# Attention and experts in one kernel: the barrier between the two parts taken out, the experts' start moved into the last batch

## What is computed

```python
x = L0_attn_x                                   # (8, 1024, 256)
xn = _layernorm(x, axis=-1)
# attention: a second layer norm of xn with ln_w, ln_b, 16 heads of 16, rotary q and k
scores = jnp.einsum('bhqd,bhkd->bhqk', q, k) / jnp.sqrt(jnp.float32(hd))
attn = jax.nn.softmax(scores, axis=-1)
out = jnp.einsum('bhqk,bhkd->bhqd', attn, v)
attention = xn + out.transpose(0, 2, 1, 3).reshape(B, N, D) @ Wo.T + bo
# experts: each of 8 experts takes its 256 best rows of each batch
affinity = jax.nn.softmax(jnp.einsum('bsd,de->bse', xn, gate_w), axis=-1)
gating, index = jax.lax.top_k(jnp.transpose(affinity, (0, 2, 1)), K)
h = jax.nn.silu(x_sel @ Wg[e]) * (x_sel @ Wu[e])          # x_sel: the rows taken, of xn
x_out = jnp.zeros_like(xn).at[b_idx, index].add((h @ Wd[e]) * gating[..., None])
return x + attention + x_out
```

## Time and profile before

| what | value |
|---|---|
| time, median of 3 runs | 1924.89 us (1923.93 to 1927.3) |
| time of the profiled execution | 1923.88 us |
| its span in the trace | 1922.1 us |
| PE busy (share of the span) | 90% |
| ACT busy | 62% |
| DVE busy | 56% |
| POOL busy | 34% |
| mean granted TensorE clock | 0.96 of full speed |

### The profile page before, as it was taken

The page is one execution under the profiler, slowest core; times in us unless marked ns, Lnnn a source line. Parts: engine busy times, 40 slices in busy tenths (PEclk is TensorE's granted clock), DMA queues, the critical chain, the costliest instruction groups (busy, mean ns, idle before and its releaser), DMA issues. The chain is left out here.

```text
span 1922.1 us, 28864 instructions
## 1 busy us (share of the span) xinstructions
PE 1730.4 (90%) x11240; PEld 1016.0 (53%) x11240; DVE 1085.6 (56%) x1910; ACT 1185.1 (62%) x1390; POOL 662.6 (34%) x599
## 2 busy tenths in 40 slices
PE   2469999999999999999999998872999999999997
PEld 2323434434433444444444343232888888888886
DVE  8846457556656555654655757822545545554543
ACT  0048887887887888788788889961333333333332
POOL 3333123233132133123213311003465565556553
PEclk9669999999999999999999999995999999999999
DMA  3173475476467458447547546423344344344333
GB/s 95 66 157 64 118 151 107 104 165 132 97 162 142 95 141 150 110 125 151 125 119 152 130 98 124 70 71 103 80 91 91 61 97 89 60 96 94 57 60 33
DMA packets 115250, 203.42 MB, mean 106 GB/s; under 512 B 21008, under 2 KB 59280, under 8 KB 115088
## 3 DMA queue, kind: packets, MB, share of 16 engines
q1 hardware_dynamic: 83600, 142.48, 34.1%
q0 software_dynamic: 31488, 58.74, 14.9%
HBM read 116.22 MB, written 84.93 MB: 105 GB/s over the span
## 5 line engine op out<-in xcount | busy, mean ns | idle before, releaser
L607 ACT ACTIVATE probs<-score 128x1024 f32<-128x1024 f32 x1024 | 979.3, 1026 | 227.2 <-PE score L745 227.1
L759 PE MATMUL o_ps<-probs,v_ones 128*32 128x512 f32 x4096 | 505.3, 612 | 0.9 <-ACT probs L607 0.9
L745 PE MATMUL score<-q_stack,k_stack 50*128 50x512 f32 x2048 | 399.8, 460 | 50.1 <-ACT probs L607 40.8
L745 PEld LDWEIGHTS score<-q_stack,k_stack 50*128 50x128 f32 x2048 | 164.9, 187 | 365.0 <-ACT probs L607 298.6
L1302 ACT ACTIVATE silu<-g_ps 128x512 f32<-128x512 f32 x128 | 76.5, 598 | 333.6 <-PE g_ps L1336 333.6
L1262 POOL DMA_INDIRECT out<-y,rows_now x128 | 203.7, 1591 | 206.1 <-DVE y L1415 176.8
L759 PEld LDWEIGHTS o_ps<-probs,v_ones 128*32 128x32 f32 x4096 | 107.8, 110 | 239.4 <-issue 162.6
L542 POOL TENSOR_TENSOR square<-qk 128x512 bf16<-128x512 f32 x64 | 88.2, 1407 | 368.8 <-DVE qk L896 368.8
L1404 DVE TENSOR_TENSOR h<-u_ps,silu 128x512 f32<-128x512 f32 x128 | 88.5, 691 | 209.7 <-PE u_ps L1336 184.8
L1253 POOL DMA_INDIRECT xs<-xn_rows,rows_now x128 | 131.7, 1029 | 38.0 <-issue 29.2
L513 POOL TENSOR_SCALAR ve<-mv 128x4 f32<-128x4 f32 x32 | 7.5, 235 | 307.3 <-DVE mv L816 307.3
(11 more groups left out here) (173 smaller groups left out, 2856.9 us busy)
## 6 DMA issues: line engine op xcount, KB each, us to landing
q_parts<-parts SPq DMA_DIRECT2D x16, 1024.0 KB, 4.3
k_parts<-parts SPq DMA_DIRECT2D x16, 1024.0 KB, 6.9
q_stack<-q_parts SPq DMA_DIRECT2D x64, 256.0 KB, 7.3
k_stack<-k_parts SPq DMA_DIRECT2D x64, 256.0 KB, 9.6
xin<-in_x POOLq DMA_DIRECT2D x16, 512.0 KB, 6.2
xn_rows<-xn POOLq DMA_DIRECT2D x16, 512.0 KB, 4.7
out<-xin POOLq DMA_DIRECT2D x16, 512.0 KB, 3.8
q_stack<-q_parts SPq DMA_DIRECT2D x64, 128.0 KB, 8.2
```

The lines of the kernel that those rows point to most:

```text
L607: act.activation(probs[probs_of(s)][:, 2 * i:2 * i + 2, :], score[ring_of(p)][:, :, :], ACT.Exp, scale=SCALE).then_inc(exp_done, 1)
L745: last = pe.matmul(score[ring_of(p)][:, w, :], k_stack[par][rows, i, kt * P:(kt + 1) * P], q_stack[par][rows, i, qh * HALF:(qh + 1) * HALF ...
L759: last = pe.matmul(o_ps[j * KEYS_W:(j + 1) * KEYS_W, :], v_ones[par][:, kt, j, :], probs[probs_of(s)][:, j, :], start=kt == 0, stop=kt == ...
```

## The change

Both parts become one function, `program`, with one block, so the engines no longer meet in the middle. The experts' tiles become views of attention tiles that are dead by then, and their PSUM banks are the attention's: `g_ps`, `u_ps`, `xt_ps` are the halves of `score` 0, 1 and 2, `d_ps` is `o_ps` and `side`. What the experts need first is put into the last batch: SP loads the first expert's weights there, ACT makes their high parts in cycles 20 to 22 and DVE the low parts in cycles 28 to 30, DVE converts the lists in cycle 25, PE transposes them as the extra job of cycle 27, and POOL gathers units 0 and 1. Batch 7's last four output projections are put at the ends of units 0 and 1. The arithmetic is the same.

```diff
-    LAST_JOBS = {0: ("top",), 9: ("wo", 0), 15: ("wo", 1), 23: ("wo", 2), 30: ("wo", 3)}
+    LAST_JOBS = {0: ("top",), 9: ("wo", 0), 15: ("wo", 1), 23: ("wo", 2), 27: ("lists",), 30: ("wo", 3)}
+    WEIGHT_CYCLE = (20, 21, 22)
+    LISTS_CYCLE = 25
+    LOW_CYCLE = (28, 29, 30)
+    END_BANKS = {("wo", q): (q // 2, q % 2) for q in range(QUARTERS)}
...
@@ SP: in the last batch, after store_o(b, 2) @@
+            else:
+                sp.wait_ge(base_out, 2 * DMA * NB)
+                sp.wait_ge(xn_out, 2 * DMA * NB)
+                sp.wait_ge(side_free, jobs.base)
+                load_weights(0)
...
@@ SP: behind the last batch @@
         load_den(NB - 1, 1)
         load_base(NB - 1)
+        sp.wait_ge(w_split, WEIGHTS)
+        load_weights(1)
         load_num(NB - 1, 1)
         spread_rec(NB - 1, 1)
         for hf in range(2):
             store_y(NB - 1, hf, end_jobs)
+        for e in range(2, E):
+            sp.wait_ge(w_split, WEIGHTS * e)
+            load_weights(e)
...
@@ POOL: behind the last batch @@
         attend(NB - 1, None, NB - 2)
+        pool.wait_ge(base_out, 2 * DMA * NB)
+        pool.wait_ge(xn_out, 2 * DMA * NB)
+        pool.wait_ge(parts_ready, 2 * NB)
+        pool.wait_ge(top_spread, 2)
+        pool.wait_ge(side_free, last_jobs.done(("lists",)))
+        gather(0)
+        gather(1)
         divide(NB - 1, 0)
-        divide(NB - 1, 1)
+        for unit in range(E * UNITS):
+            if unit + 2 < E * UNITS:
+                gather(unit + 2)
+            if unit == 0:
+                divide(NB - 1, 1)
+            scatter(unit)
...
@@ POOL: in scatter @@
+            if e == 0:
+                pool.wait_ge(y_out, 2 * DMA * (2 * bp + 2))
...
@@ ACT: in the last batch, and behind it @@
+                for m in range(WEIGHTS):
+                    if nxt is None and s == 2 * WEIGHT_CYCLE[m] + 1:
+                        act.wait_ge(side_free, last_jobs.base)
+                        high_weights(0, m)
...
+        act.wait_ge(parts_out, NB * 2 * PARTS_DMA)
+        turned(0)
+        act.wait_ge(pv_done, NB * STEPS)
+        for unit in range(E * UNITS):
+            expert_unit(unit)
...
@@ PE: behind the last batch @@
-        for s in (STEPS - 2, STEPS - 1):
-            weigh(NB - 1, s)
-        for job in END_JOBS:
-            pe.wait_ge(side_free, end_jobs.before(job))
-            run_job(end_jobs, job, None, NB - 1, side[:, :])
+        weigh(NB - 1, STEPS - 2)
+        turn(0)
+        weigh(NB - 1, STEPS - 1)
+        for unit in range(E * UNITS):
+            if unit % UNITS == 0:
+                pe.wait_ge(w_split, WEIGHTS * (unit // UNITS + 1))
+            gate_up(unit)
+            if unit + 1 < E * UNITS:
+                turn(unit + 1)
+            if unit == 0:
+                pe.wait_ge(o_copied, NB * 2 * NG)
+                pe.wait_ge(side_free, end_jobs.base)
+            down(unit)
+            for job in END_JOBS:
+                if END_BANKS[job][0] == unit:
+                    pe.wait_ge(x_split, DC * (unit + 1) + END_BANKS[job][1] + 1)
+                    run_job(end_jobs, job, None, NB - 1, xt_ps[END_BANKS[job][1]])
...
@@ DVE: in the last batch, and behind it @@
+                    if c == LISTS_CYCLE:
+                        order_lists()
...
+                if nxt is None and c in LOW_CYCLE:
+                    if c == LOW_CYCLE[0]:
+                        dve.wait_ge(parts_out, NB * 2 * PARTS_DMA)
+                    low_weights(0, LOW_CYCLE.index(c))
...
         copy_o(NB - 1, 2 * NG - 1)
-        for qh in range(2):
-            if qh == 1:
-                invert(NB - 1, 1)
-            for i in range(2):
-                quarter_split(NB - 1, 2 * qh + i)
-            for i in range(2):
-                take(end_jobs, ("wo", 2 * qh + i), None, NB - 1, side[:, :])
+        turned(0)
+        for unit in range(E * UNITS):
+            expert_unit(unit)
...
@@ DVE: in expert_unit @@
+                if unit == 0 and f == 1:
+                    invert(NB - 1, 1)
+            low(unit, FC - 1)
+            if unit + 1 < E * UNITS:
+                turned(unit + 1)
+            if unit < 2:
+                quarter_split(NB - 1, 2 * unit)
+                quarter_split(NB - 1, 2 * unit + 1)
...
@@ the new helpers that these call @@
+        def low_weights(e, m):
+            dve.wait_ge(w_high, WEIGHTS * e + m + 1)
+            dve.tensor_tensor(we_lo[e % 2][m], w_raw[m], we_hi[e % 2][m], ALU.subtract).then_inc(w_split, 1)
...
+        def high_weights(e, m):
+            act.wait_ge(w_in, WEIGHTS * DMA * (e + 1))
+            act.copy(we_hi[e % 2][m], w_raw[m]).then_inc(w_high, 1)
...
+        def turn_lists(bank):
+            pe.wait_ge(row_added, 3)
+            for i, src in enumerate((row_f, gate_f)):
+                for half in range(HALVES):
+                    at = (HALVES * i + half) * LISTS
+                    last = pe.transpose(bank[:, at:at + LISTS], src[:, half * P:(half + 1) * P], ident_sb[:, :])
+            return last
```

463 lines of the change are left out of this document (191 added, 272 removed).

## The result

The changed kernel took 1880.96 us (median of 4 runs, 1877.44 to 1884.39) beside 1926.1 us of the kernel before (1923.93 to 1928.88): a ratio of 0.976, 95% interval 0.9742 to 0.9778. The forecast was 1876 us, with a range of 1871 to 1885. The median fell by 45.1 us; the sum had said 48.6. (The kernel before has one more run here than it had at the forecast, when its median was 1924.89 us.) In the profiled executions, which can be taken apart, the span fell by 42.9 us, 5.7 short of the sum. The join was forecast to the tenth of a microsecond. Of the 5.7 us, 2.5 lie in the batches ahead of it, 2.5 in the units from unit 3 on, 0.5 in unit 0 and 0.4 in units 1 and 2; the smaller terms gave back 0.3.

What follows compares the result with a forecast made beforehand. PE was taken to bound the kernel, busy 90% of 1922.1 us, except in the 57.0 us join. Terms summed to -48.6 us, giving a 1873.5 us span, 1875.3 with the time around it, forecast as 1876 (range 1871 to 1885).

Steps and rivals of the forecast that it cites:

- the sum: All terms added: -57.0 + 2.1 + 2.6 + 5.8 - 2.15 + 0.1 = -48.6 us.
- The join: Between last `weigh` and first gate matmul: 57.0 us taken out, 2.1 us of DVE's copy and low parts left.
- The casts: ACT's three weight casts in cycles 20 to 22 of the last batch: 2.6 us added, between 2.4 and 2.94.
- The output projections: Four projections moved onto PE's path at the ends of units 0 and 1: 5.8 us added.
- The clock at unit 0: Unit 0 starts at full clock after the short hole, taking 17.65 us instead of 19.80: -2.15 us.
- a short fall of the clock: Rival: PE begins unit 0 at half clock after the 2.1 us hole, costing 2.15 us, so 1878; chance 0.13.
- A unit takes 17.65 us: Expert units from unit 3 on: the prediction is wrong if any takes anything but 17.65 us.
- a wait of PE for a split in units 0 to 3: Sign in the first expert units: if PE waits for a split there, the prediction is wrong.
- The batches ahead: Attention batches before the join: no change forecast; about half of 1.0 us added for the profiled execution lying below the median.
- The queues: Second half's way round beside units 0 and 1, with POOL and DVE work queued behind: costed at nothing.
- backed-up queues: Rival in units 0 to 3: slow transfers and a late chain cost PE 2 to 9 us, 1878 to 1885; chance 0.14.
- The late rows: Rival: the first gather starts only at the last batch's end, 8.5 to 11 us back, 1884 to 1886; chance 0.06.

Runs made afterwards that it cites:

- late gather: Changed kernel with POOL's first gather of expert rows waiting until PE has done all weighs of the last batch but the last: 1894.08 us, ratio 0.9831.
- 160 bytes: Changed kernel with 160 bytes of padding per partition behind zn_lo, run twice: 1881.19 us (ratio 0.9759) and 1879.22 us (0.9737).
- 416 bytes: Changed kernel with 416 bytes of padding per partition behind zn_lo: 1877.4 us, ratio 0.974 to the kernel before.
- 32 bytes: Changed kernel with 32 bytes of padding ahead of the second tile of parts, which holds the rows, and 32 behind it: 1884.74 us, ratio 0.9775.
- control: The changed kernel itself, unedited, run once more beside three edited kernels on one chip: 1878.54 us, ratio 0.9752.

## Why the forecast was nearly right, step by step

**The join, -57.0 and +2.1 us.** Right, both to 0.1 us. The three pieces of the gap (0.07, 0.69, 1.28 and the reaction) were those of the earlier trace rows. The two kernels with another order on DVE show that most of the gap was not needed: 0.74 us is left when `copy_o` is out of it.

**The casts, +2.6 us.** The number came out, 2.47 us between the same marks in the profiles compared, but with luck. From the mark to the end of the last `weigh`, the nine kernels with the casts on ACT and no late gather fall into two kinds. Three of them took 131.0 us, with the clock at 1.00 throughout. Six, the changed kernel among them, took 131.9 to 132.5 us, and in each the clock fell once while the casts ran. The three with the casts on POOL took 129.5 to 129.6 us and the kernel before 129.40, none with a fall. So the casts themselves cost 1.4 to 1.6 us, under the forecast's lower end of 2.4, and a fall of the clock beside them another 0.9 to 1.5. The same 20 us in the changed kernel and in the changed kernel again (columns as in the earlier trace rows):

```profile
1239.00:1259.00 20.00, 17.90 (x118) 6.62 (x112) 13.26 (x30) 18.85 (x21) 0.00 (x0) 0.91 0.04 9
1239.00:1259.00 20.00, 17.62 (x128) 6.51 (x120) 14.79 (x34) 19.41 (x21) 0.00 (x0) 1.00 0.06 14
```

The step that was wrong is the wait that the casts absorb: the forecast allowed 0.54 us of it. In the changed kernel run again ACT stood idle for 8.1 us from the mark to the last `weigh`, against 9.0 in the kernel with POOL's casts and no padding. That is 0.9 us of waits absorbed. The rest of the difference was not traced. Whether the casts bring the fall about isn't shown either; it came in seven of the ten profiles with casts on ACT, the late gather included, and in none of the four without. One `cast` itself took 1.05 us, about as in the earlier trace rows:

```profile
1242.11 1.05 ACT L706 CAST zn_hi<-xin 128x1024 fp32r<-128x1024 f32 x1
1243.05 3.78 ACT L737 ACTIVATE probs<-score 128x1024 f32<-128x1024 f32 x4
1246.67 1.08 ACT L706 CAST zn_hi<-xn 128x1024 fp32r<-128x1024 f32 x1
```

**The output projections, +5.8 us.** Right: the pair behind unit 0 took 2.84 us, 5.7 us for the four, and doubling them added 5.5 in the profile. `turn(1)` to `turn(3)` grew by 6.24 us all the same: the rest is 0.4 us of slower even experts and the 0.2 us that PE lost behind DVE's low part.

**The clock at unit 0, -2.15 us.** The direction was right and the size was not. `gate_up(0)` gave back 1.64 us in the profiled execution; it would have been 1.90 but for the 0.26 us that an even expert's `gate_up` now takes more. Part of the miss is a reading of the rows. The chain's row of unit 1 starts at 1362.83 us, but PE's timeline of the kernel before has that first gate matmul at 1362.67. Unit 0 had lost 1.99 us there (12.90 - 10.91), not 2.15. And the fall came back in some profiles: of the nine with a gap of 2.1 us and no late gather, three show it (12.6 to 12.8 us to `turn(1)` instead of 11.0 to 11.3). That is the rival "a short fall of the clock", which had 0.13: it came true in a third of the profiles, at about 1.6 us. In neither profile with a gap of 0.74 us did it fall. The nine are of seven kernels. Both profiles with 160 bytes alone have the fall and neither of the changed kernel does, so whether it goes by the execution or by the edit isn't shown. The Trainium skill ("TensorE: Matmul & The Clock Gate", section "What's actually happening") says that the same kernel can see the change at another place in another run. The two profiles of the changed kernel agree in batch 7 and ahead of it: the first has a fall beside the casts and a long batch 6, the second has neither.

**"A unit takes 17.65 us": the term that was mis-sized.** The forecast named it as what would prove it wrong. Units of even experts took 17.82 to 17.92 us. `gate_up` of an even expert took 0.26 us more (11.17 - 10.91), the unit as a whole about 0.18, since what is behind `gate_up` took 6.66 us there and 6.74 in the others. `turn(3)` to `turn(31)`, with 13 such units, is 2.5 us longer than before, and with units 0, 1 and 2 it comes to some 3.0 us. The other sign that was named, a wait of PE for a split in units 0 to 3, came true too, by the 0.7 us in `down(1)`. The cause is where tiles lie in memory: in the joined program weights and rows share the attention's tiles, and the gate matmuls have a pitch of 227 ns if both kinds lie at the same place modulo 256 bytes, and of 232 to 233 ns at the other distances tried. Three edits that only move tiles show it from both sides: 160 or 416 bytes made the slow units fast, 32 bytes made the fast ones slow. How the chip comes to it stays open. `parts0`, which holds two of the six parts of an even expert's weights (one of the four that `gate_up` reads), was at the same place modulo 256 as the rows in the changed kernel, and its matmuls were followed after 234 and 235 ns, as slow as those beside them. So it isn't a matter of one matmul's own two operands. Nor are all matmuls of a slow expert slow: by their place in a slice the means over its units at full clock go from 226.5 to 237.3 ns.

**The batches ahead, +2.5 us.** The forecast took the profiled execution of before as the base and added half a microsecond. Nothing was changed there, and the mark of the same program stood at 1159.15 and at 1155.87 us. The stretch ahead of it goes in steps: from a batch to the next it is 147.1 us, or about 1.65 or 3.3 us more. The granted clock goes with it: in a batch of 147.1 us it fell to half speed for a short while once, in one of 148.8 twice, in one of 150.4 three times. These are batches 2, 4 and 6 of the changed kernel, and batch 6 of the kernel before (from first `weigh` to first `weigh`; PE's busy time alone):

```profile
416.40:567.10 150.70, 145.33 (x994) 0.97 0.58 129
715.80:862.90 147.10, 142.02 (x990) 0.99 0.57 129
1010.20:1160.60 150.40, 146.03 (x995) 0.97 0.56 125
```

```profile
1010.80:1158.10 147.30, 142.91 (x998) 0.99 0.59 129
```

Batch 6 is where the changed kernel lost what it lacks at the mark: 150.4 us against 147.3. Over the fourteen profiles the time from the first `weigh` of batch 1 to the mark goes from 883.7 us with 8 such falls to 894.3 us with 14, some 1.7 us for each. What sets how many there are in an execution wasn't found. It is why the padding can't be seen in the median: 2.9 to 3.9 us less in the units in each of the three profiles with 160 or 416 bytes alone, but medians 1.1 us below the control's (416 bytes) and 0.7 above (160), for the two that ran beside it. In the two profiles with 160 bytes alone, four and three batches of 150.4 us came (in the changed kernel two and one of over 150), and the clock fell at unit 0 in both. Whether the padding makes such falls likelier, or this was chance, is open.

**The queues.** No rival of backed-up queues came true, but the slacks were smaller than forecast. The load of the numerators started at 1310.05 us, SP could issue the load behind the reciprocals' store only 5.2 us after it, and the second `divide` started at 1322.43 us, not 1315.8:

```profile
1296.62 0.55 SPq L452 DMA_DIRECT2D den<-o_sums  x1
1310.05 1.21 SPq L459 DMA_DIRECT2D num<-o_sums  x2
1311.31 0.46 SPq L471 DMA_DIRECT2D den_recs<-den_rec  x1
1316.48 1.20 SPq L476 DMA_DIRECT2D rec<-den_recs  x2
```

DVE came to the second splits at 1328.70 us, 3.9 us behind the end of the `divide` (forecast 7), and PE turned the rows of unit 3 at 1345.92 us, when the last of their gathers had been issued by 1338.87; with 2.7 us to land that is a slack of 4 us, not 9. Of the 6.6 us by which the `divide` was late, 3.0 are the splits' (their end at 1310.0 us, not 1307.0, of which 2.4 since unit 0 started at 1293.12 and not at 1290.7), which moves DVE's and PE's requests too; the other 3.6 are the way from the store's issue to the `divide`, 11.1 us beside units 0 and 1 and not 7.5, and they came out of the slack. That is the 11 us up to which the forecast said the slacks hold.

**The late rows,** 0.06: they were in time, and the run without the cover shows that the price, 8.5 to 11 us, was too low only by the clock's share: 12.1 us in the profiles compared (9.6 up to the last `weigh`, 2.6 in `gate_up(0)` at the lower clock).

## What to carry to other kernels

When two phases are joined, the work moved under the last cycles of the first costs what it adds on the engine that never rests there, so give it to the engine that does: three casts on ACT cost 1.4 to 1.6 us, and 2.5 to 3.1 where the clock fell beside them, on POOL 0.1 to 0.2. What lies between the last matmul of one phase and the first of the next is worth ordering by hand down to single instructions, for the gap itself and because behind a gap of 2.1 us the clock fell in three of nine profiles, and behind one of 0.74 us in neither of two. And a joined program has another memory layout: compare the time of identical units before and after, and where matmuls of one shape differ by 2% by tile only, try the tiles' places modulo 256 bytes.

## What was unexpected in the hardware

Matmuls of 128x512 in fp32r had a pitch of 226.7 to 227.5 ns or of 232.1 to 233.2 ns by the places of the tiles (means by kernel and kind of expert over units at full clock), as told above. A DVE instruction of 0.68 us that reads SBUF alone took 2.27 us beside one of POOL of 2.41 us, and one that reads PSUM kept its 0.69 us beside the same. An execution of unchanged batches differs from another by whole steps of 1.65 or 3.3 us a batch, one step for each further short fall of the clock, 11 us at the mark between the earliest and the latest profile.
